# A graph kernel's third aggregation: run totals kept as linear rows and written to their nodes by POOL during the decoder

## The reference

```
def gcn_conv(x, edge_index, W, b, n_nodes):
    xw = x @ W
    norm = dis[row] * dis[col]
    msg = xw[row] * norm[:, None]
    agg = jax.ops.segment_sum(msg, col, num_segments=n_nodes)
    return agg + b
z = jax.nn.relu(gcn_conv(x, edge_index, W_enc1, b_enc1, n))
z = jax.nn.relu(gcn_conv(z, edge_index, W_enc2, b_enc2, n))   # 64 wide: the "third aggregation"
z = jax.nn.relu(z @ W_dec1 + b_dec1)
x_hat = z @ W_dec2 + b_dec2
```

## Time and profile before

| what | value |
|---|---|
| median of three runs | 8635.45 us (8628.08 to 8637.53) |
| profiled execution, its own time | 8638.8 us |
| its span | 8637.1 us |
| busy: PE, DVE, ACT, POOL | 3652.6, 5444.9, 2663.1, 5223.9 us |
| stage 3, first gather to the next stage's first load | 5526.98 to 6551.76 us |
| decoder, to the next stage's first operation | 6551.76 to 7073.60 us |

### The profile page before, as it was taken

The page is one execution under the profiler, slowest core; times in us unless marked ns, Lnnn a source line. Parts: engine busy times, 40 slices in busy tenths (PEclk is TensorE's granted clock), DMA queues, the critical chain, the costliest instruction groups (busy, mean ns, idle before and its releaser), DMA issues. The chain is left out here.

```text
span 8637.1 us, 110883 instructions
## 1 busy us (share of the span) xinstructions
PE 3652.6 (42%) x20396; PEld 2793.2 (32%) x20396; DVE 5444.9 (63%) x22718; ACT 2663.1 (31%) x6456; POOL 5223.9 (60%) x4583
## 2 busy tenths in 40 slices
PE   7103555555669999800001776400005863333100
PEld 1002333334658888700000555300004652222100
DVE  8766555557998999755556999511115666666654
ACT  0671000005663333222222666300002334444322
POOL 0005888884437777777775222477775457777577
PEclk9556566667889999955555888655557985555555
DMA  8894333337983333333335888400006973333343
GB/s 229 316 358 118 41 41 41 41 41 206 274 249 88 94 93 95 87 95 94 95 93 152 291 287 287 136 22 22 21 22 196 306 238 104 104 104 104 101 139 119
DMA packets 1050252, 1197.22 MB, mean 139 GB/s; under 512 B 205970, under 2 KB 868830, under 8 KB 1039671
## 3 DMA queue, kind: packets, MB, share of 16 engines
q1 hardware_dynamic: 861252, 937.39, 34.3%
q0 software_dynamic: 188928, 259.09, 13.7%
HBM read 642.13 MB, written 581.54 MB: 142 GB/s over the span
## 5 line engine op out<-in xcount | busy, mean ns | idle before, releaser
L665 ACT ACTIVATE dense<-dense,nbi,sc 128x128 f32<-128x128 f32 x2370 | 936.5, 482 | 239.6 <-DVE nbi L1203 168.0
L536 POOL DMA_INDIRECT dense<-t_xs,gidx x784 | 778.7, 993 | 266.5 <-issue 235.4
L406 POOL DMA_INDIRECT g<-t_src,gidx x398 | 398.1, 1000 | 774.1 <-DVE keyr L440 653.1
L1519 PE MATMUL ps<-w,dense 128*128 128x128 f32 x6272 | 807.7, 282 | 0.0
L552 DVE TENSOR_SCALAR sidx<-keyend 128x2 int32 (+1 forms) x784 | 138.0, 176 | 985.8 <-DMA dense<-t_y,gidx 805.0
L1519 PEld LDWEIGHTS ps<-w,dense 128*128 128x128 f32 x6272 | 732.8, 192 | 47.6 <-issue 0.4
L424 POOL DMA_INDIRECT t_acc<-tot,sidx x392 | 638.5, 1629 | 146.5 <-issue 129.9
L570 PE MATMUL ps<-tot,share 128*128 128x128 f32 x4 | 1.5, 487 | 1532.2 <-DVE tot L559 1532.2
L938 POOL TENSOR_TENSOR dense<-dense 128x1280 f32<-128x1280 f32 (+1 forms) x79 | 229.1, 2900 | 596.4 <-ACT dense L665 596.4
L1249 DVE SCALAR_TENSOR_TENSOR dense<-xT 128x256 f32<-128x256 f32 x1568 | 545.5, 418 | 30.3 <-ACT xT L1673 21.5
L483 PE MATMUL ps<-ident,keyr 128*128 128x128 f32 x394 | 118.5, 399 | 1047.8 <-DVE seq L453 600.3
(11 more groups left out here) (261 smaller groups left out, 12570.3 us busy)
## 6 DMA issues: line engine op xcount, KB each, us to landing
dense<-t_xs SPq DMA_DIRECT2D x78, 1320.0 KB, 6.3
dense<-in_x SPq DMA_DIRECT2D x156, 640.0 KB, 5.5
t_xs<-dense SPq DMA_DIRECT2D x98, 528.0 KB, 7.4
t_xs<-hb SPq DMA_DIRECT2D x78, 660.0 KB, 5.0
t_sum<-dense SPq DMA_DIRECT2D x98, 512.0 KB, 3.5
t_src<-dense SPq DMA_DIRECT2D x78, 640.0 KB, 4.0
t_acc<-dense SPq DMA_DIRECT2D x78, 640.0 KB, 5.2
dense<-t_acc SPq DMA_DIRECT2D x78, 640.0 KB, 5.9
```

The source lines that it names most:

```text
L406: gp.indirect_dma_start(rows[:, p.k, c, :], None, table, bass.IndirectOffsetOnAxis(ap=gidx[:, p.k, c:c + 1], axis=0)) \
L536: gp.indirect_dma_start(rows[:, p.k, c, :], None, table, bass.IndirectOffsetOnAxis(ap=gidx[:, p.k, c:c + 1], axis=0)) \
L665: i = nc.scalar.activation(out_t[0:p, k, 0:D], in_t[0:p, k, :], ACT.Relu, bias=bias[0:p, k:k + 1], scale=scale[0:p, k:k + 1])
L1519: i = nc.tensor.matmul(ps[:, o:o + P], xm[:, p.w, k, c * P:(c + 1) * P], w1[:, k, :], start=False, stop=(k == R - 1))
```

## The change

The totals of stage 3 are no longer written to their nodes there. SP stores each pair's `toty` as it stands into a new table `t_run3`, one row per edge in the order of edges (`keep_runs3`). `run_sums` waits for that store in place of the indirect write and makes no `sidx`. The rest of a run that crosses partitions is added to one row of `t_run3` (`carry_pool`), with a matrix `carry` that also keeps only the partition in which the run ends.

In the decoder POOL walks over 49 groups of 1,024 edges (`late_pool`): it loads a group's rows linearly, copies its eight key columns, writes eight columns with indirect DMAs into `t_yacc`, and counts a group as written when they have landed. SP's `dec_sums` reads from a small table `need` how many groups hold targets below the block's end, and waits for that count ahead of the loads. The bias row is added by DVE (`dec_bias`) two blocks behind `dec_scale`, and not by POOL. The keys are made once in E0 at pair 1 (`keys_late`), turned round through memory by SP (`t_key` to `keyg`), and `need` at pair 8 (`needs`).

```diff
+GROUP = 8
+GE = GROUP * P
+NGROUP = T * P // GE
+FULL = E // GE
...
+        t_run3 = dram("t_run3", (T * P + P, H2))
+        t_key = dram("t_key", (T * P,), I32)
...
+        gs3 = dense[:, 9 * KD:9 * KD + SLOTS * GROUP * H2].rearrange("p (u c f) -> p u c f", u=SLOTS, c=GROUP)
+        below = dense[0:1, 0:(NB + 1) * NGROUP].rearrange("p (b g) -> p b g", b=NB + 1)
...
+        def late_pool(gp, s, runs, target, rows):
+            def load(r, u):
+                if needed(r):
+                    gp.wait_ge(s["scat"][u].sem, s["scat"][u].after(r * 16 * GROUP))
+                    gp.sem_inc(tick, 1)
+                gp.dma_start(rows[:, u, :, :].rearrange("p c f -> p (c f)"),
+                             runs[bass.ds((r * SLOTS + u) * GE, GE), :].rearrange("(p c) f -> p (c f)", c=GROUP)) \
+                    .then_inc(s["load"][u].sem, 16)
+                gp.tensor_copy(gq[:, u, :], keyg[:, bass.ds((r * SLOTS + u) * GROUP, GROUP)]).then_inc(s["index"].sem, 1)
+            def write(r, u):
+                gp.wait_ge(s["index"].sem, s["index"].after(r * SLOTS + u + 1))
+                gp.sem_inc(tick, 1)
+                gp.wait_ge(s["load"][u].sem, s["load"][u].after(r * 16 + 16))
+                gp.sem_inc(tick, 1)
+                for c in range(GROUP):
+                    gp.indirect_dma_start(target, bass.IndirectOffsetOnAxis(ap=gq[:, u, c:c + 1], axis=0),
+                                          rows[:, u, c, :], None, bounds_check=N - 1, oob_is_err=False) \
+                        .then_inc(s["scat"][u].sem, 16)
+            def landed(r, u):
+                gp.wait_ge(s["scat"][u].sem, s["scat"][u].after((r + 1) * 16 * GROUP))
+                gp.sem_inc(s["written"].sem, 1)
+            group_loop(gp, (load, 0), (write, 1), (landed, 2))
...
+        def carry_pool(gp, s, z, runs, total):
+            for k in range(RING):
+                gp.wait_ge(s["keep"][k].sem, s["keep"][k].after(16 * uses(k)))
+            gp.wait_ge(z["total"].sem, z["total"].after(1))
+            gp.sem_inc(tick, 1)
+            gp.indirect_dma_start(runs, bass.IndirectOffsetOnAxis(ap=firsti[:, 0:1], axis=0), total, None,
+                                  compute_op=ALU.add).then_inc(z["last"].sem, 16)
+            gp.wait_ge(z["last"].sem, z["last"].after(16))
...
-        def run_sums(v, s, p, totals, in0, in1, per=1):
+        def run_sums(v, s, p, totals, in0, in1, per=1, free="scat"):
             width = in0.shape[-1]
             if needed(p.n):
-                v.wait_ge(s["scat"][p.k].sem, s["scat"][p.k].after(p.n * 32))
-            nc.vector.tensor_scalar(sidx[:, p.k, :], keyend[:, bass.ds(p.q * 2, 2)], float(per), None, ALU.mult)
+                v.wait_ge(s[free][p.k].sem, s[free][p.k].after(p.n * (32 if per else 16)))
+            if per:
+                nc.vector.tensor_scalar(sidx[:, p.k, :], keyend[:, bass.ds(p.q * 2, 2)], float(per), None, ALU.mult)
...
-            nc.tensor.matmul(ps[:, SUMS:SUMS + width], share[:, :], totals[:, (NPAIR - 1) % RING, 1, 0:width],
+            nc.tensor.matmul(ps[:, SUMS:SUMS + width], joined[:, :], totals[:, (NPAIR - 1) % RING, 1, 0:width],
...
+            sp.dma_start(nexti[0:LASTP - 1, :], dst[T:LASTP * T].rearrange("(p t) -> p t", t=T)[:, 0:2]) \
+                .then_inc(S0["ldk"].sem, 16)
...
+            sp.wait_ge(C0["keys"].sem, C0["keys"].after(1))
+            sp.dma_start(t_key.rearrange("(p t) -> p t", t=T), keyi[:, :]).then_inc(C0["kept"].sem, 16)
+            sp.wait_ge(C0["kept"].sem, C0["kept"].after(16))
+            sp.dma_start(keyg.rearrange("p (g c) -> p g c", c=GROUP), t_key.rearrange("(g p c) -> p g c", p=P, c=GROUP)) \
+                .then_inc(C0["kept"].sem, 16)
+            sp.wait_ge(C0["kept"].sem, C0["kept"].after(32))
...
+            def keep_runs3(p):
+                sp.wait_ge(R3["second"].sem, R3["second"].after(p.q + 1))
+                sp.dma_start(t_run3[0:T * P, :].rearrange("(p t) f -> p t f", t=T)[:, bass.ds(p.q * 2, 2), :],
+                             toty[:, p.k, :, :]).then_inc(R3["keep"][p.k].sem, 16)
+            pair_loop(sp, (keep_runs3, 0))
...
             def dec_sums(r, u, p):
                 b = r * SLOTS + u
                 if needed(b - SLOTS + 1):
                     sp.wait_ge(L3["tr"].sem, L3["tr"].after(b - SLOTS + 1))
+                    sp.sem_inc(tock, 1)
+                groups = sp.value_load(need[0:1, bass.ds(b, 1)], min_val=1, max_val=NGROUP)
+                sp.wait_ge(G3["written"].sem, G3["written"].after(groups))
+                sp.sem_inc(tock, 1)
                 sp.dma_start(yin[u][0:p], rows_of(t_yacc, b, p)).then_inc(L3["lda"][u].sem, 16)
                 sp.dma_start(yown[u][0:p], rows_of(t_y, b, p)).then_inc(L3["lda"][u].sem, 16)
...
             gath3 = rows_pool(gp, E3, t_y, gy)
-            ends3, close3 = run_pool(gp, R3, R3["second"], t_yacc, toty, Z3, msg[:, 0, 0, 0:H2])
-            pair_loop(gp, (gath3, 0), (ends3, 3))
-            close3()
+            pair_loop(gp, (gath3, 0))
+            carry_pool(gp, R3, Z3, t_run3, msg[:, 0, 0, 0:H2])
             end_phase(gp, PO)
-
-            def dec_xb(r, u, p):
-                b = r * SLOTS + u
-                gp.wait_ge(L3["ld"][u].sem, L3["ld"][u].after(r * 16 + 16))
-                gp.tensor_tensor(xin[u][0:p], xin[u][0:p], bd2b[0:p, :].rearrange("p (a f) -> p a f", a=1)
-                                 .to_broadcast([p, K, D]), ALU.add).then_inc(L3["xb"].sem, 1)
-            node_loop(gp, (dec_xb, 0))
+            late_pool(gp, G3, t_run3, t_yacc, gs3)
...
+            def keys_late():
+                vec = nc.vector
+                v.wait_ge(S0["ldk"].sem, S0["ldk"].after(16 * 4))
+                chain(vec.tensor_copy(nextf[:, 0:1], nexti[:, 0:1]))
+                chain(vec.tensor_tensor(nextf[:, 1:2], nextf[:, 0:1], dst_f[:, T - 1:T], ALU.is_equal))
+                vec.tensor_scalar(ta[:, 0:T - 1], keyend[:, 0:T - 1], 1.0, None, ALU.mult)
+                chain(vec.scalar_tensor_tensor(out=ta[:, T - 1:T], in0=nextf[:, 1:2], scalar=float(2 * NR),
+                                               in1=dst_f[:, T - 1:T], op0=ALU.mult, op1=ALU.add))
+                vec.tensor_scalar(keyi[:, :], ta[:, :], 1.0, None, ALU.mult).then_inc(C0["keys"].sem, 1)
+                chain(vec.tensor_scalar(tb[:, :], ta[:, :], float(2 * NR), float(2 * T * P), ALU.is_ge, ALU.mult))
+                chain(vec.tensor_tensor(tb[:, :], tb[:, :], tcv[:, :], ALU.add))
+                vec.tensor_reduce(nextf[:, 2:3], tb[:, :], AX.X, ALU.min)
+                chain(vec.tensor_scalar(nextf[:, 3:4], spare[:, 0:1], float(T * P - N), None, ALU.add))
+                vec.tensor_tensor(firsti[:, 0:1], nextf[:, 2:3], nextf[:, 3:4], ALU.min)
...
+            def needs():
+                vec = nc.vector
+                chain(vec.tensor_copy(firstf[:, :], firstd[:, :, 0]))
+                chain(vec.tensor_tensor(below, firstf.rearrange("p (a g) -> p a g", a=1).to_broadcast([1, NB + 1, NGROUP]),
+                                        limits.rearrange("p (b a) -> p b a", a=1).to_broadcast([1, NB + 1, NGROUP]),
+                                        ALU.is_lt))
+                chain(vec.tensor_reduce(needf[:, :], below, AX.X, ALU.add))
+                vec.tensor_scalar(need[:, :], needf[:, :], 1.0, None, ALU.max)
...
+                if isinstance(pair.q, int) and pair.q == 1:
+                    keys_late()
+                if isinstance(pair.q, int) and pair.q == 8:
+                    needs()
...
-                run_sums(v, R3, p, toty, gy[:, p.k, 0, :], gy[:, p.k, 1, :])
+                run_sums(v, R3, p, toty, gy[:, p.k, 0, :], gy[:, p.k, 1, :], 0, "keep")
...
+            def dec_bias(r, u, p):
+                v.wait_ge(L3["ld"][u].sem, L3["ld"][u].after(r * 16 + 16))
+                nc.vector.tensor_tensor(xin[u][0:p], xin[u][0:p], bd2b[0:p, :].rearrange("p (a f) -> p a f", a=1)
+                                        .to_broadcast([p, K, D]), ALU.add).then_inc(L3["xb"].sem, 1)
...
-            node_loop(v, (dec_scale, 0), (dec_x3, 3))
+            node_loop(v, (dec_scale, 0), (dec_bias, 2), (dec_x3, 3))
...
-            run_close_tensor(pe, R3, Z3, toty, H2)
+            run_close_tensor(pe, R3, Z3, toty, H2, carry)
```

More of the change, by code:

```diff
@@ L105, in node_loop, with group_loop, at @@
         at(b)
+def group_loop(eng, *stages):
+    most = max(lag for _, lag in stages)
+    peeled = (SLOTS + most + SLOTS - 1) // SLOTS
+    def at(g):
+        for fn, lag in stages:
+            if 0 <= g - lag < NGROUP:
+                fn((g - lag) // SLOTS, (g - lag) % SLOTS)
+    for g in range(peeled * SLOTS):
+        at(g)
+    with eng.Fori(peeled, NGROUP // SLOTS) as r:
+        for u in range(SLOTS):
+            for fn, lag in stages:
+                back = (lag - u + SLOTS - 1) // SLOTS if lag > u else 0
+                fn(r - back if back else r, u - lag + back * SLOTS)
+    for g in range(NGROUP // SLOTS * SLOTS, NGROUP + most):
+        at(g)
 class Pair:
```

(23 more changed lines are left out.)

35 lines of the change are left out of this document (29 added, 6 removed).

## The result

The changed kernel takes 8340.4 us (median of 4 runs, 8327.1 to 8345.1) where the kernel before takes 8636.5 on the same chip: a ratio of 0.9653, 95% interval 0.9636 to 0.9670, 296 us less. The prediction said 8410 (8325 to 8550).

| stretch | before | after | difference | predicted |
|---|---|---|---|---|
| up to stage 3 | 5526.98 | 5521.18 | -5.8 | +10 |
| stage 3 | 1024.8 | 505.8 | -519.0 | -519 |
| decoder | 521.8 | 737.0 | +215.2 | +284 |
| behind the decoder | 1563.5 | 1570.3 | +6.8 | 0 |

A forecast was written before the change was run, and what follows sets the result against it. Stage 3 was bound by POOL issuing 784 indirect DMAs, the decoder by an SP-DVE loop with DMA close behind. Terms -519 + 284 + 10 = -225 us gave 8414 profiled, 8410 median; range 8325 to 8550.

The forecast's parts named there:

- Stage 3: Stage 3: POOL keeps only 392 gathers at 1.26 us each, so 1024.8 us becomes 506, -519 us.
- The close: End of stage 3, after the last gather: landing, totals, store, indirect add and barrier, 12 us where it was 9.3.
- How early POOL is done: Decoder: POOL takes 12.1 us a group, G groups counted at 1.6 + 12.1 (G + 1) us, all 49 about 605.
- One rival: Decoder: the loop lengthens or POOL is held more; R = 8.5 gives +358 us, 8483 in all; chance 20%.
- The hold: Decoder: DVE products with two SBUF inputs delay POOL's DMAs by 1.2 us a block, bounds 0 and 3.2.
- The decoder's own pace: Decoder blocks no longer slowed by POOL's groups: R = 7.2 us a block, bounds 6.33 and 8.5.
- a loop of 7.0: Decoder's SP-DVE loop over two blocks, with bias and register read added: (12.06 + 1.48 + 0.4) / 2 = 7.0 us a block.
- a memory of 7.3: Decoder's DMA limit with POOL's groups beside it: 5.8 / (0.92 - 0.13) = 7.3 us a block.
- The formula of the prediction: Decoder's last load: largest over b of group-writing time plus R (78 - b), 777 us; with the tail 806, +284.
- crossing: Decoder: block from which its own pace, not POOL's groups, sets the time; largest sum flat around b = 29.
- E0 and setup: E0 and setup: `needs` +6, SP's turn of the keys +3, small operations +1, `keys_late` nothing: +10 us.
- POOL unhindered, decoder at its old pace: Rival for the decoder: R = 6.33 and no hold, stage 728 us, +207, total 8328; chance 17%.

The follow-up runs named there:

- the second run: The changed kernel unchanged, run once more beside the kernel before on a fast chip: 8336.8 us beside 8641.3, ratio 0.9651.
- the last experiment: Changed kernel with the decoder waiting for all 49 groups, by a constant without the register read; slow chip, against the kernel before: 9728.5 us, ratio 1.0053.

## Why the prediction was right, and where it was off

**Stage 3: right to a microsecond, partly by luck.** 505.8 us against 506. The gathers take 489.2 us and not 494, at 1.25 us each where 1.26 was taken. The close, from the last gather's end (6010.37) to the decoder's first operation (6026.98), takes 16.6 us and not 12: POOL's indirect add starts 6.7 us after the last gather where 4.7 was counted, and 8.3 us lie behind it and not 5.7. The two errors cancel. SP's 196 stores are hidden. POOL waits 61 us for DVE's index, where before it waited 47 for DVE, but the idle time ahead of the gathers is the same in sum (140.1 us, before 140.2): these short waits take the place of "issue" and do not add to it.

**How early POOL is done: two terms too large.** The group was put at 12.1 us unhindered and takes 10.89 (6041.41 to 6052.30 in the rows above; 10.71 in the version that overlaps nothing, taken over its 49 row loads as with the others). I had taken 1.27 us for the linear load; it takes 0.59 with no 0.30 us behind it, and the copy 0.20. And "load, write and landing are one turn apart, so G groups are counted at 1.6 + 12.1 (G + 1)" was wrong by a whole turn: the count does not wait for POOL to reach its place in the program. Both together: the first block goes out at 70.1 us where 86 was forecast, SP's last wait for POOL ends 284 us in and not at about 400, and the last group's writes begin at 6614.0, 587 us in, and not at 690. One rival has a slip here: its 304 us at b = 16 counts 24 groups where the formula gives 23. Redone over all blocks its largest sum is 848 and not 850, which changes nothing.

**The hold: right size, now with its cause.** 1.2 us a block was taken. Over the stage the writes lost (1114 - 974) x 392 = 55 us and the copies (360 - 204) x 49 = 8, and 60 blocks had their products while POOL wrote: 1.05 us a block. Of the 392 writes 95 were held, 1.6 a block, as the "one or two starts" of the prediction had it. The Trainium skill ("SBUF — State Buffer", section on SBUF's two separate sides) says that a DVE operation with two SBUF inputs and a GpSimd operation that reads SBUF lock a shared port pair against each other. The runs agree: with the bias add gone 1025 ns, with one of its inputs in PSUM 1019, with no DVE work at all 974. The 1.48 us operation makes most of the hold. What remains, 45 to 51 ns a write, is that of the two of 0.83 us: no run took them away, but in the trace of the moved bias the writes that start inside them take 1247 and 1396 ns, and those that start anywhere else 972 to 988. The traffic beside POOL adds nothing that shows.

**The decoder's own pace: right value, a mixed reason.** 7.2 was taken as the larger of a loop of 7.0 and a memory of 7.3; measured 6.91 (6.85 in the second run). With POOL silent the averages are 6.33 before, 6.87 with the bias on DVE and 7.01 with the read as well, and the loop's forecast was 7.0. That is close in part by luck: the forecast started from one pair of blocks at 12.06 us, 6.03 each, where the mean was 6.33, and it counted 0.2 us a block for the register read, which costs 0.03 (7.01 against 6.98). The 7.3 of memory was not reached either: the blocks ran at 6.91 with POOL's traffic beside most of them. Nor does the bias keep its 0.74 under traffic, where it cost 0.16. The read, taken at its likely place on the loop, takes this long (min, median, max ns):

```profile
L941 SPq TENSOR_LOAD <-need x79: 262/491/1735, 6027.0 to 6738.5; - x79
```

The Trainium skill ("DMA: Bandwidth & Descriptors", latency and other measured facts) gives such a load a floor of about 600 ns; here 491 ns is the median and 262 the least. With either figure the pace does not move, since taking the read away changed it by 0.03 us.

**The sum.** The formula of the prediction has its maximum at b = 29, 777 us. The measured crossing is at b = 16: 283.8 + 62 x 6.91 = 712 us. Of the 65 us between them 27 are POOL's earlier count at b = 16 (1.6 + 12.1 x 24 + 1.2 x 16 = 311 against 283.8), 18 the pace (62 x 0.29), and 20 that the maximum no longer lies at b = 29. The tail is 24.7 us and not 29. By stages, the profiled execution is 78 us below the forecast: 69 in the decoder, 16 ahead of stage 3, and 7 the other way behind the decoder. Those 7 lie in A3, whose 784 gathers have means of 951 and 973 ns where they had 944 and 959; its second run shows it too, and the cause stays open.

**E0 and setup.** +10 was forecast, -5.8 stands in the table. The needs' product does what the earlier trace rows say of such products: here DVE's product, POOL's gather beside it (3.96 us where its neighbour takes 1.02) and DVE's reduction, in order of time.

```profile
783.33 4.18 DVE L1287 TENSOR_TENSOR dense<-firstf,limits 1x3871 f32<-1x3871 f32 x1
...
784.41 3.96 POOL L450 DMA_INDIRECT g<-t_src,gidx  x1 [0.30 <-issue]
787.54 4.17 DVE L1290 TENSOR_REDUCE needf<-dense 1x79 f32<-1x3871 f32 x1
```

Its price at that pair is 3 us. The total of this stretch cannot be told from chance: code that is the same up to there, but for one constant in the last, reaches stage 3's first gather at 5521.0, 5522.6, 5523.4 and 5518.4 us in four of the runs.

**The rival that came nearest** was "POOL unhindered, decoder at its old pace", 8328. It has 12.1 us a group and no hold, where 10.9 and the hold make about 12, and a pace of 6.33 where 6.91 was measured; a crossing at b = 29 that was not there makes up for the pace. It was near by errors that cancel, and nearer than the forecast itself (12 us off, and 70).

## What to carry to other kernels

Work that one engine does alone can be moved beside a stage that another resource bounds, and the price is then the order: ask which consumer needs the most producers first. Here the densest nodes came first and that wait took 110 us; taking both lists from the other end gave back 88. When the moved engine becomes the bound, look for what holds it: letting a two-input DVE operation work on one operand in PSUM instead of SBUF gave another 41 us, and gave nothing while POOL was not the bound.

## What was not expected of the hardware

**POOL's queue runs ahead of POOL.** A wait and a count placed behind eight indirect writes were passed 8.7 us before POOL began the last of them (6042.6 against 6051.32). Where a count stands in the program is not when it happens; a wait placed so that it is reached with nothing left to run, as in the run that counts a group in the turn in which it is written, does stop POOL, 3.4 us a group.

**A linear load from POOL is cheap.** 0.59 us and no gap behind it, where an indirect write has 0.97 and 0.30.

**One decoder, two paces.** In the version that overlaps nothing a block takes 7.2 us, and the residual's load lands 6.6 us after its issue; in the changed kernel, with POOL writing, 6.85 and 5.2, and behind POOL's last group 6.7 and 5.1. So the decoder with more traffic beside it is the faster one. Landings (median us at the line's end) with POOL silent throughout, then in the changed kernel's second run from 6600 to 6730 us:

```profile
dense<-t_x SPq DMA_DIRECT2D x67, 640.0 KB, 6.6
out_rows<-dense SPq DMA_DIRECT2D x67, 640.0 KB, 7.5
```

```profile
dense<-t_x SPq DMA_DIRECT2D x19, 640.0 KB, 5.1
out_rows<-dense SPq DMA_DIRECT2D x19, 640.0 KB, 6.1
```

But POOL's traffic is not what makes it fast, for the same code with the memory to itself settles in either of two rhythms. In the last experiment a block takes 6.79 us between blocks 9 and 24, and 7.27 from there on. In the kernel before with the bias on DVE it takes 6.53 us between blocks 16 and 29, with a DMA share of 0.92 and landings of the residual at 5.0 us, and 7.28 from block 36 on, with 0.82 and 6.6. What picks the rhythm stays open.

**On the slow chips TensorE stood idle for no visible reason.** In the version without the bias, blocks of 37 to 53 us stand beside a DMA share of 0.24 to 0.30 while POOL writes. TensorE's waits there, from 6900 to 7240 us:

```profile
PE ps L1746 <- DVE dense L1520: 98.6, 5, 29.9
PE ps L1736 <- issue: 58.5, 6, 13.7
PE ps L1746 <- issue: 52.3, 3, 19.4
PE ps L1724 <- issue: 25.1, 10, 6.9
```

"Issue" is a wait for nothing that the profile shows. TensorE has none on the fast chips in the same code, and none on the slow chip once POOL is done. In the version that waits for each group's landing, on the same slow chip, it has 4.0 us of them. That POOL's traffic delays the others' instructions there is the reading that fits; no run shows it, and why two of the chips behave so is open. What the changed kernel does on them was not measured.
